# A per-batch weight pick, matmul and residual add: loads moved to GpSimd as one packet per DMA engine, stores to SyncE, weight picks to ScalarE

## The reference

```python
B, C, D, T, N_SUBJECTS = (128, 128, 128, 1024, 8)
w = weights[subjects]
out = jnp.einsum('bct,bcd->bdt', x, w)
return x + out
```

## Time and profile before

| | before |
|---|---|
| median of 3 runs | 330.94 us (330.94 to 331.13) |
| span of the profiled execution | 329.6 us |
| PE busy | 240.7 us, 73% |
| DVE busy | 156.7 us, 48% |
| POOL busy | 37.7 us, 11% |
| mean rate of the DMA engines | 409 GB/s |
| bytes moved | 134.87 MB |

### The profile page before, as it was taken

How to read it: one execution, slowest core, us unless ns; L and a number is a source line. 1 busy time by engine, 2 the same in 40 slices (tenths; PEclk the granted TensorE clock), 3 DMA queues, 4 the chain that set the end, 5 groups by cost and what they waited for, 6 DMA issues and landing times.

```text
span 329.6 us, 2144 instructions
## 1 busy us (share of the span) xinstructions
PE 240.7 (73%) x512; PEld 94.4 (29%) x512; DVE 156.7 (48%) x128; POOL 37.7 (11%) x132
## 2 busy tenths in 40 slices
PE   2987768667786986776776777876866866866880
PEld 1432323223332332232232232232332322322330
DVE  0564454454354544545545445445445445445451
POOL 1332234443333100000000000000000000000000
PEclk9999999999799899999999999999999999999997
DMA  7999999999999999999999999999999999999996
GB/s 266 331 381 420 421 421 421 421 421 419 421 421 420 420 420 421 419 421 421 421 420 421 421 421 420 421 418 421 420 421 421 421 421 419 422 421 421 421 417 253
DMA packets 35933, 134.87 MB, mean 409 GB/s; under 512 B 2129, under 2 KB 3154, under 8 KB 35922
## 3 DMA queue, kind: packets, MB, share of 16 engines
q1 hardware_dynamic: 18480, 67.64, 50.7%
q10 hardware_dynamic: 17442, 67.11, 49.7%
HBM read 67.63 MB, written 67.11 MB: 409 GB/s over the span
## 4 chain that ended last, share of the span: by engine, by line
DMA 69%; PE 22%; DVE 6%; issue 1%; POOLq 0%; POOL 0%
DMA x_ring<-x 68%; PE product L99 22%; DVE x_ring L111 6%; DMA weight_bank<-weights 1%; POOLq L83 0%; POOLq L84 0%; POOL weight_of_batch L84 0%; POOLq L80 0%
## 5 line engine op out<-in xcount | busy, mean ns | idle before, releaser
L99 PE MATMUL product<-x_ring,weight_of_batch 128*128 128x512 f32 x512 | 240.7, 616 | 81.3 <-DMA x_ring<-x 74.7
L111 DVE TENSOR_TENSOR x_ring<-product,x_ring 128x1024 f32<-128x1024 f32 x128 | 156.7, 1225 | 166.6 <-PE product L99 166.6
L99 PEld LDWEIGHTS product<-x_ring,weight_of_batch 128*128 128x128 f32 x512 | 94.4, 193 | 226.8 <-DMA x_ring<-x 129.8
L84 POOL COPY weight_of_batch<-weight_bank 128x128 f32 x128 | 37.5, 293 | 72.1 <-issue 72.1
L130 POOL MEMSET const-float32-0.0<- 128x1 f32 x1 | 0.1, 98 | 0.2 <-issue 0.2
L130 POOL MEMSET const-bfloat16-1.0<- 128x1 bf16 x1 | 0.1, 101 | 0.0
L130 POOL MEMSET const-uint8-127<- 128x1 uint8 x1 | 0.1, 101 | 0.0
L130 POOL MEMSET const-float32-1.0<- 128x1 f32 x1 | 0.1, 98 | 0.0
## 6 DMA issues: line engine op xcount, KB each, us to landing
x_ring<-x SPq DMA_DIRECT2D x62, 1024.0 KB, 14.9
out<-x_ring ACTq DMA_DIRECT2D x62, 1024.0 KB, 13.0
x_ring<-x SPq DMA_DIRECT2D x4, 512.0 KB, 8.1
out<-x_ring ACTq DMA_DIRECT2D x4, 512.0 KB, 5.8
weight_bank<-weights SPq DMA_DIRECT2D x1, 512.0 KB, 4.4
subject_row<-subjects ACTq DMA_DIRECT2D x1, 0.5 KB
```

The lines of the kernel that those rows point to most:

```text
L84: pool.tensor_copy(weight_of_batch[:, b, :], weight_bank[:, bass.ds(subject, 1), :]).then_inc(picked, 1)
L99: last = pe.matmul(product[b % PRODUCTS][:, cols], weight_of_batch[:, b, :], x_ring[:, slot, k, cols], start=True, stop=True)
L111: dve.tensor_tensor(x_ring[:, slot, k, :], product[b % PRODUCTS][:, :], x_ring[:, slot, k, :], mybir.AluOpType.add).then_inc(added, 1)
```

## The change

The batches now form 64 equal tiles of two; the tiles of one batch at the start and the end are gone. GpSimd issues the loads, each with `single_packet=True`, and waits for nothing but the store of the slot's last tile; the wait for the tile four before is gone. SyncE still issues the transfer of the matrices first, and then the stores. ScalarE loads the subject numbers and picks the weights, two batches of a tile with one increment of `picked`, into a ring of 16 places instead of 128; so a pick waits for the matmuls of the tile eight before. The programs of TensorE and ScalarE are loops of eight laps over the eight slots, with semaphore waits against register values. TensorE multiplies a whole tile of four PSUM banks, with two such products instead of four of half the size, and VectorE adds a whole tile of 2048 columns with one instruction.

```diff
@@ -18,109 +6,108 @@
 PSUM_BANK_COLS = 512
 PSUM_BANKS = 8
 DMA_INC = 16
-def tile_batches(n_batches, per_tile, ramp):
-    middle = n_batches - 2 * sum(ramp)
-    counts = list(ramp) + [per_tile] * (middle // per_tile) + list(ramp)[::-1]
-    assert sum(counts) == n_batches
-    firsts = np.cumsum([0] + counts[:-1]).tolist()
-    return list(zip(firsts, counts))
+PER_TILE = 2
+SLOTS = 8
 def subject_residual_kernel(nc, x, subjects, weights, out):
     f32, i32 = mybir.dt.float32, mybir.dt.int32
     B, C, T = x.shape
     S, _, D = weights.shape
     assert C == D == nc.NUM_PARTITIONS
-    PER_TILE = 2
-    SLOTS = 8
-    AHEAD = 4
-    TILES = tile_batches(B, PER_TILE, ramp=[1, 1])
+    TILES = B // PER_TILE
+    LAPS = TILES // SLOTS
+    LAP_BATCHES = SLOTS * PER_TILE
     BANKS = T // PSUM_BANK_COLS
-    PRODUCTS = PSUM_BANKS // BANKS
-    INDEX_LOAD = 8
+    PRODUCTS = PSUM_BANKS // (BANKS * PER_TILE)
+    x_of_tile = x.rearrange("(n k) c t -> n c k t", k=PER_TILE)
+    out_of_tile = out.rearrange("(n k) c t -> n c k t", k=PER_TILE)
     with ExitStack() as ctx:
         x_ring = ctx.enter_context(nc.sbuf_tensor("x_ring", [C, SLOTS, PER_TILE, T], f32))
         weight_bank = ctx.enter_context(nc.sbuf_tensor("weight_bank", [C, S, D], f32))
-        weight_of_batch = ctx.enter_context(nc.sbuf_tensor("weight_of_batch", [C, B, D], f32))
+        weight_ring = ctx.enter_context(nc.sbuf_tensor("weight_ring", [C, LAP_BATCHES, D], f32))
         subject_row = ctx.enter_context(nc.sbuf_tensor("subject_row", [1, B], i32))
-        product = [ctx.enter_context(nc.psum_tensor(f"product{i}", [D, T], f32)) for i in range(PRODUCTS)]
+        product = [ctx.enter_context(nc.psum_tensor(f"product{i}", [D, PER_TILE, T], f32)) for i in range(PRODUCTS)]
...
         x_in = [ctx.enter_context(nc.semaphore(f"x_in{s}")) for s in range(SLOTS)]
         x_out = [ctx.enter_context(nc.semaphore(f"x_out{s}")) for s in range(SLOTS)]
         picked = ctx.enter_context(nc.semaphore("picked"))
         multiplied = ctx.enter_context(nc.semaphore("multiplied"))
         added = ctx.enter_context(nc.semaphore("added"))
         block = ctx.enter_context(nc.Block())
+        @block.gpsimd
+        def _(pool):
+            for t in range(TILES):
+                slot, lap = t % SLOTS, t // SLOTS
+                if lap:
+                    pool.wait_ge(x_out[slot], DMA_INC * lap)
+                pool.dma_start(x_ring[:, slot, :, :], x_of_tile[t], single_packet=True).then_inc(x_in[slot], DMA_INC)
         @block.sync
         def _(sp):
             sp.dma_start(weight_bank[:, :, :], weights.rearrange("s c d -> c s d")).then_inc(weights_in, DMA_INC)
-            for t, (first, count) in enumerate(TILES):
-                slot, lap = t % SLOTS, t // SLOTS
-                if t >= AHEAD:
-                    sp.wait_ge(added, sum(TILES[t - AHEAD]))
-                if lap:
-                    sp.wait_ge(x_out[slot], DMA_INC * lap)
-                sp.dma_start(x_ring[:, slot, 0:count, :],
-                             x[first:first + count, :, :].rearrange("b c t -> c b t")).then_inc(x_in[slot], DMA_INC)
-        @block.gpsimd
-        def _(pool):
-            pool.wait_ge(subjects_in, DMA_INC)
-            pool.wait_ge(weights_in, DMA_INC)
-            for b in range(B):
-                subject = pool.value_load(subject_row[0:1, b:b + 1], min_val=0, max_val=S - 1)
-                pool.tensor_copy(weight_of_batch[:, b, :],
-                                 weight_bank[:, bass.ds(subject, 1), :]).then_inc(picked, 1)
+            for t in range(TILES):
+                slot = t % SLOTS
+                sp.wait_ge(added, PRODUCTS + t + 1)
+                sp.dma_start(out_of_tile[t], x_ring[:, slot, :, :]).then_inc(x_out[slot], DMA_INC)
+            for slot in range(SLOTS):
+                sp.wait_ge(x_out[slot], DMA_INC * LAPS)
         @block.tensor
         def _(pe):
-            for t, (first, count) in enumerate(TILES):
-                slot, lap = t % SLOTS, t // SLOTS
-                pe.wait_ge(x_in[slot], DMA_INC * (lap + 1))
-                for k in range(count):
-                    b = first + k
-                    pe.wait_ge(picked, b + 1)
-                    if b >= PRODUCTS:
-                        pe.wait_ge(added, b - PRODUCTS + 1)
-                    for n in range(BANKS):
-                        cols = slice(n * PSUM_BANK_COLS, (n + 1) * PSUM_BANK_COLS)
-                        last = pe.matmul(product[b % PRODUCTS][:, cols], weight_of_batch[:, b, :],
-                                         x_ring[:, slot, k, cols], start=True, stop=True)
+            pe.sem_inc(multiplied, SLOTS)
+            with pe.Fori(0, LAPS) as lap:
+                for slot in range(SLOTS):
+                    pe.wait_ge(picked, lap * SLOTS + (slot + 1))
+                    pe.wait_ge(added, lap * SLOTS + (slot + 1))
+                    pe.wait_ge(x_in[slot], lap * DMA_INC + DMA_INC)
+                    for k in range(PER_TILE):
+                        for n in range(BANKS):
+                            cols = slice(n * PSUM_BANK_COLS, (n + 1) * PSUM_BANK_COLS)
+                            last = pe.matmul(product[slot % PRODUCTS][:, k, cols],
+                                             weight_ring[:, slot * PER_TILE + k, :],
+                                             x_ring[:, slot, k, cols], start=True, stop=True)
                     last.then_inc(multiplied, 1)
         @block.vector
         def _(dve):
-            for t, (first, count) in enumerate(TILES):
+            dve.sem_inc(added, PRODUCTS)
+            for t in range(TILES):
                 slot = t % SLOTS
-                for k in range(count):
-                    b = first + k
-                    dve.wait_ge(multiplied, b + 1)
-                    dve.tensor_tensor(x_ring[:, slot, k, :], product[b % PRODUCTS][:, :], x_ring[:, slot, k, :],
-                                      mybir.AluOpType.add).then_inc(added, 1)
+                dve.wait_ge(multiplied, SLOTS + t + 1)
+                dve.tensor_tensor(x_ring[:, slot, :, :], product[t % PRODUCTS][:, :, :], x_ring[:, slot, :, :],
+                                  mybir.AluOpType.add).then_inc(added, 1)
         @block.scalar
         def _(act):
             act.dma_start(subject_row[0:1, :], subjects.rearrange("(one b) -> one b", one=1)).then_inc(subjects_in, DMA_INC)
-            for t, (first, count) in enumerate(TILES):
-                slot = t % SLOTS
-                act.wait_ge(added, first + count)
-                act.dma_start(out[first:first + count, :, :].rearrange("b c t -> c b t"),
-                              x_ring[:, slot, 0:count, :]).then_inc(x_out[slot], DMA_INC)
-            for slot in range(SLOTS):
-                act.wait_ge(x_out[slot], DMA_INC * len(range(slot, len(TILES), SLOTS)))
+            act.wait_ge(subjects_in, DMA_INC)
+            act.wait_ge(weights_in, DMA_INC)
+            with act.Fori(0, LAPS) as lap:
+                for slot in range(SLOTS):
+                    act.wait_ge(multiplied, lap * SLOTS + (slot + 1))
+                    for k in range(PER_TILE):
+                        n = slot * PER_TILE + k
+                        subject = act.value_load(subject_row[0:1, bass.ds(lap * LAP_BATCHES + n, 1)],
+                                                 min_val=0, max_val=S - 1)
+                        copied = act.copy(weight_ring[:, n, :], weight_bank[:, bass.ds(subject, 1), :])
+                    copied.then_inc(picked, 1)
 def kernel(x, itok_B_0_7, L0_cond_weights):
```

## The result

The changed kernel takes 327.86 us (median of 4 runs, 327.53 to 327.99) beside 331.03 us of the kernel before (330.94 to 331.3). The ratio is 0.9902, with a 95% interval of 0.9888 to 0.9916: 1% faster. The profiled execution took 327.53 us, with a span of 325.4 us, the shortest of the four (325.4, 325.7, 325.9 and 325.9). The changed kernel takes 2.1 us more than its span. The kernel before, where both were taken of one execution, takes 1.8 us more, not the 1.3 of the comparison of a median with another execution's span.

The account below looks back on a forecast made before the run. The prediction took the DMA engines, full at 421 GB/s in the middle, as the bound. It summed 330.9 - 2.0 (gate) - 2.5 (packets) + 0.5 (POOL's issue) = 326.9 us, range 323 to 339.5, the forecast's own 323 to 329.

Parts of the forecast that it names:

- the gate: Loads at the start no longer wait for the tile four before: 1.7 us at 10 to 14 us plus 0.3, together 2.0.
- rival 3: At the DMA engines the flag changes nothing, so only the 2.0 us gain and 0.5 us cost stay: 329.4 us; chance 0.10.
- One packet per engine: POOL's loads become 16 packets instead of 256, saving fixed cost per packet: 2.5 us taken, 7.6 us at most.
- POOL's later first load: At the start, POOL pays more to issue a load than SP did: a cost of 0.5 us, bounds 0 and 1.
- The end: After the last stores, the last data to the end of the span stay as before: 3.1 us.
- Picks, loops and whole adds: ACT's picks, PE's loop and DVE's adds of 2048 columns lie under the queue of four tiles: 0 us.
- The slot's life of 40 us: In the middle, eight slots at 4.98 us a tile give each slot 40 us, against 19 us without queueing.
- Rival 1: At the start, weight packets wait behind 64 KB load packets; weights land at 24 us, time 339 us; chance 0.28.
- Rivals 2 to 4: Second: POOL's loads move more slowly, 335.3 us at worst, chance 0.12; fourth: PE becomes the bound, 375 us, chance 0.02.

Follow-up runs that it names:

- experiment 1: The kernel before with only the gate of four tiles taken away: 329.05 us, ratio 0.9935.
- experiment 5: The changed kernel with the weights issued only when the subject numbers have landed: 334.62 us with single_packet, 335.06 us without.
- experiment 7: The kernel before without its gate and with equal tiles in place of single batches at both ends: 328.69 us.

## Why the prediction was right or wrong

The forecast of 326.9 us lay 1.0 us below the 327.86 measured. The direction and the mechanism named first, the gate, were right. The largest term, that of the packets, was not: rival 3, that the flag changes nothing, had a chance of 0.10 and is what happened. That the time still came near is partly luck, since the rest of the gain was one that I had not forecast: the end, and a cost of POOL that was not there.

- **The gate, 2.0 us.** Right: 2.1 us by experiment 1. I had taken 0.3 of the 0.8 us lost at 16 to 20 us. In experiment 1 the 0.8 us there are gone, but 0.6 are lost at 12 to 16, part of it new. The windows from 10 to 20 us gave 1.8 us in all, so beside the hole of 1.7 only some 0.1 was won there.
- **One packet per engine, 2.5 us.** Wrong, it is 0. The line through two packet sizes gave a fixed cost of 7.9 ns, but the step from "each packet has a fixed cost" to "the flag removes it" was not supported by a row. The middle stands at 421 GB/s with and without the flag, and experiment 5 fits engines that change queues at 4 KB either way. The saving by the Trainium skill's 3 cycles (DMA: Bandwidth & Descriptors, Why small descriptors are slow), estimated at 3.4 us, is not seen in any run here. That section of the Trainium skill also says that joining is worth it only for descriptors of up to 256 B, which the prediction left out, and pieces of 4 KB agree with it.
- **POOL's later first load, a cost of 0.5 us.** Wrong by that much: the window of 2 to 4 us moved 250 GB/s against 213. The 0.2 us between them are no gain of POOL either. From 0 to 4 us the rate is 131 and 122 GB/s in the two profiles of the changed kernel, and 125 in experiment 1, where SP issues the loads behind the weights as before. The cost is nothing that these runs can tell.
- **The end, 3.1 us kept.** Wrong in size. From 320 us to the end 1.8 us were lost in the first profile, and 2.5 us in the second profile of the same kernel, against 3.3 before. This is what offset a good part of the missing packet term.

  The traces show where it lies. Each transfer ends with 16 increments of its semaphore, which I take as one for each DMA engine. The median one of these 16, for the last store, comes at 326.5 us in the kernel before and at 323.9 to 324.3 us in all ten profiles of kernels without the gate on which the weights are not late, experiment 1 among them. The last increment follows the median by 2.4 us before, 2.5 in experiment 1, 1.1 and 2.0 in the two profiles of the changed kernel, and 0.9 to 2.2 in the others. So the gate alone brought the middle engine's end forward; what differs beyond it in the spans is mainly how far the last engine lags, and the lag is there already in the middle of the run (2.5 us in experiment 1, 0.8 in the changed kernel, 100 to 200 us). Why it lags stays open.
- **Picks, loops and whole adds at 0.** Right within what the runs can tell, and the reason given fits: the queue of waiting stores covers them. It also covered the table loads, eight times 1.28 us, that I had not foreseen. The whole first tile and its whole add delay the first store by 4.9 us; only the full start covers that.
- **The slot's life of 40 us** came out as 39.3, as it must with a full ring.
- **Rival 1, the starved weights.** Its mechanism exists, with another unit. I had one weight packet wait for 64 KB; it waits for about 4 KB. The rule of the Trainium skill that an engine takes turns by whole packets (DMA: Bandwidth & Descriptors, Queues, rings and completion order) agrees with experiment 5 if the packet is one piece of 4 KB or a few; the 9 to 17 descriptors that the Trainium skill calls typical there are not seen. Whether the flag formed a larger packet that was split again, or none, stays open. It did not strike because the weights were issued 0.5 us ahead of POOL's first load. When that load's first piece starts, at 3.57 us, 715 of the 1024 weight rows have started; the other 309, 19 for each engine, pass in 0.65 us beside 23 pieces, without the turns of experiment 5, where too some 24 rows an engine went ahead of them. The run with 1.2 us of delay is the measure of how near it was. The point from which it costs, a landing at 11 us, was about right: a landing at 15.5 us cost 6.8 us where 4.5 follow from the distance, and the table load may be 1.3 of the rest.
- **Rivals 2 to 4.** The middle did not slow, PE did not become the bound (3.7 us a tile in the chain). Rival 3, that the flag changes nothing, gave 329.4 and is what happened at the engines; 0.5 of the other 1.5 us are POOL's cost that did not come, and the rest is the end and steps too small to tell.

What remains is small. From experiment 7 to the changed kernel there are 0.7 us (328.69 to 328.0), made of steps of 0.1 to 0.4 us (issuing engines, loop, whole adds) that are as large as the spread of the runs. No single one of them is shown. From experiment 1 to the changed kernel, single batches included, it is 1.1 us, clear of the spread as a whole, and by the increments above it is mainly the smaller lag of the last DMA engine. No kernel tried here beat the changed one by more than that spread. With 320.1 us of bytes at 421 GB/s in a span of 325.4, only the first 4 us and the end are left to win.

## What to carry to other kernels

When the DMA engines are full in the middle, look only at the first and the last microseconds: count what each window lost against the full rate, and ask which wait emptied the queue there. Before a shorter end is put down to the change, profile the same kernel twice: here the end alone moved by 0.7 us between two profiles. A gate that limits how far loads run ahead costs nothing in the middle and 2 to 6 us at the start, depending on how late the first result is. A small transfer that the first computation needs must be issued before the bulk, not merely early: a delay of 1.2 us at issue made it land 10.7 us later.

## What the runs showed of the hardware

- Two queues on one DMA engine take turns by pieces, not by bytes: in 6 us 541 rows of 512 B passed beside 544 pieces of 4 KB, after a start in which some 24 rows of each engine went ahead. The 64 rows of an engine landed after 13.5 us, against 4.0 us when they were ahead of the loads. `single_packet` on POOL's loads did not change that.
- With ACT's copies inside a loop there is a table load at the head of each lap, 1283 ns, eight in all; POOL's copies before had none. No run has ACT's program written out, so that the loop is the cause is not shown.
- POOL is busy 713 ns for each load it issues, eight in a row in 5.8 us, fast enough to keep ahead of 2.5 us a tile.
- The DMA engines do not end together. The window after the last full one, in the kernel before without its gate and in the second profile of the changed kernel:

```profile
322.00:324.00 2.00, 0.00 (x0) 0.00 (x0) 0.00 (x0) 0.00 (x0) 0.50 0.93 381
324.00:326.00 2.00, 0.00 (x0) 0.00 (x0) 0.00 (x0) 0.00 (x0) 0.50 0.24 98
```

```profile
322.00:324.00 2.00, 0.00 (x0) 0.00 (x0) 0.00 (x0) 0.00 (x0) 0.00 (x0) 0.50 0.88 360
324.00:326.00 2.00, 0.00 (x0) 0.00 (x0) 0.00 (x0) 0.00 (x0) 0.00 (x0) 0.50 0.13 53
```

One to two microseconds at a falling rate close every profile, and their length differs between executions of one kernel: the last increment of the last store comes 1.1 us after the median one in one profile of the changed kernel and 2.0 us in the other. What makes some engines end later was not found out.
